# Reading, adding and storing seven of sixteen token groups during the last expert tiles of a fused perceiver layer

## The reference, cut to what matters

```python
logits = flat @ router_w.T
topk_scores, topk_idx = jax.lax.top_k(logits + router_bias, 2)
topk_scores = softmax(topk_scores)
hidden = silu(gate_all) * up_all                    # 16 experts of 128 hidden units
out = einsum('nk,nkd->nd', combine, down_all)       # two experts a token
out = out + (silu(flat @ sh_gate.T) * (flat @ sh_up.T)) @ sh_down.T
x = x + out
```

## Time and profile before

| | |
|---|---|
| median of 3 runs | 538.88 us (538.51 to 539.96) |
| profiled execution, its own time | 540.22 us |
| its span, first to last instruction | 538.5 us |
| PE / DVE / ACT / POOL busy | 498.2 / 399.3 / 200.1 / 198.0 us |
| chain that ended last | PE 70%, DVE 9%, DMA 8%, POOL 5% |
| mean granted clock of PE | 0.976 |

### The profile page before, as it was taken

The page is one execution under the profiler, slowest core; times in us unless marked ns, Lnnn a source line. Parts: engine busy times, 40 slices in busy tenths (PEclk is TensorE's granted clock), DMA queues, the critical chain, the costliest instruction groups (busy, mean ns, idle before and its releaser), DMA issues.

```text
span 538.5 us, 14453 instructions
## 1 busy us (share of the span) xinstructions
PE 498.2 (93%) x5012; PEld 348.7 (65%) x5013; DVE 399.3 (74%) x1068; ACT 200.1 (37%) x617; POOL 198.0 (37%) x314
## 2 busy tenths in 40 slices
PE   7988899999999999999989999999979899999950
PEld 7765566656666666666655667766735578888840
DVE  3699599999999999999653588888775325555545
ACT  2343323433223333333221366666341035555500
POOL 4000412212221112221222576766766616655620
PEclk9999999999999999999999999999998979999995
DMA  7999688877998888885215999710122245554249
GB/s 276 356 352 243 189 279 291 251 209 252 294 304 286 279 279 272 256 273 196 66 40 165 253 309 297 205 52 2 50 89 90 89 115 157 159 150 120 74 165 302
DMA packets 67348, 108.83 MB, mean 202 GB/s; under 512 B 8115, under 2 KB 49125, under 8 KB 67304
## 3 DMA queue, kind: packets, MB, share of 16 engines
q1 hardware_dynamic: 60888, 97.83, 58.6%
q0 software_dynamic: 3792, 8.43, 4.5%
q10 hardware_dynamic: 2624, 1.97, 1.2%
HBM read 85.31 MB, written 24.85 MB: 205 GB/s over the span
## 4 chain that ended last, share of the span: by engine, by line
PE 70%; DVE 9%; DMA 8%; POOL 5%; issue 4%; ACT 1%; SPq 1%; POOLq 0%; DVEq 0%; ACTq 0%
PE banks L1110 15%; PE banks L1134 15%; PE banks L1516 8%; DMA ring<-in_ctx_dram 5%; POOL rows_by_expert L727 4%; PE banks L1528 4%; PE banks L1122 3%; DVE ctxT L1638 3%; PE banks L1147 3%; PE banks L1069 2%; PE banks L1510 2%; DMA xn_all<-expert_out 2%; PE banks L1243 2%; PE banks L1295 2%; PE banks L1155 2%
## 5 line engine op out<-in xcount | busy, mean ns | idle before, releaser
L1638 DVE STREAM_TRANSPOSE ctxT<-ring 128x832 f32<-128x832 f32 x128 | 121.7, 1009 | 4.2 <-DMA ring<-in_ctx_dram 4.1
L1110 PE MATMUL banks<-ctxT,qT_all 32*64 32x416 f32 (+2 forms) x2048 | 93.9, 498 | 2.5 <-issue 2.1
L1134 PE MATMUL banks<-ring,prob 128*64 128x256 f32 (+1 forms) x832 | 93.6, 381 | 0.7 <-ACT prob L839 0.7
L1134 PEld LDWEIGHTS banks<-ring,prob 128*64 128x64 f32 (+1 forms) x832 | 58.6, 137 | 31.5 <-issue 4.2
L1110 PEld LDWEIGHTS banks<-ctxT,qT_all 32*64 32x64 f32 x2048 | 56.8, 131 | 31.2 <-issue 14.0
L638 POOL TENSOR_TENSOR var<-mv,eps 128x1 f32<-128x1 f32 x32 | 6.3, 196 | 168.6 <-DVE mv L1683 116.5
L761 POOL DMA_INDIRECT expert_out<-prob,dest x47 | 46.2, 984 | 41.6 <-DVE prob L2099 27.7
L852 ACT ACTIVATE prob<-banks,negmax 128x416 f32<-128x416 f32 (+2 forms) x80 | 41.1, 531 | 30.2 <-DVE negmax L1660 30.2
L1516 PE MATMUL banks<-ring,ctxT 128*128 x188 | 50.7, 394 | 0.1
L674 POOL TENSOR_TENSOR ctxT<-ctxT,k_mask 128x1088 f32<-128x1088 f32 x16 | 33.1, 2069 | 25.3 <-ACT ctxT L930 25.3
L839 ACT COPY prob<-banks 128x512 f32<-128x512 f32 x64 | 27.7, 514 | 38.0 <-PE banks L1122 37.9
(11 more groups left out here) (269 smaller groups left out, 940.5 us busy)
## 6 DMA issues: line engine op xcount, KB each, us to landing
ring<-in_ctx_dram SPq DMA_DIRECT2D x48, 1024.0 KB
qT_all<-q_by_pair SPq DMA_DIRECT2D x56, 128.0 KB, 8.9
rows_by_expert<-blank SPq DMA_DIRECT2D x8, 774.0 KB, 7.2
ctxT<-rows_by_expert SPq DMA_DIRECT2D x47, 129.0 KB, 2.1
mid<-stage SPq DMA_DIRECT2D x31, 128.0 KB, 2.3
ring<-in_ctx_dram SPq DMA_DIRECT2D x16, 130.0 KB
ctxT<-mid SPq DMA_DIRECT2D x16, 128.0 KB, 4.5
qT_all<-mid SPq DMA_DIRECT2D x16, 128.0 KB, 4.9
```

Source lines behind the costliest of these rows:

```text
L1110: last = pe.matmul(S[a][64 * b:64 * b + 64, 0:KW[a]], q_rep[mine, r, c, 64 * b:64 * b + 64], ctxT[mine, c, b, 0:KW[a]], start=c == 0, stop ...
L1134: last = pe.matmul(U[64 * b:64 * b + 64, 0:D], probT[0:rows, k, 64 * b:64 * b + 64], ring[0:rows, r, b, k, :], start=k == 0, stop=k == KT)
L1638: dve.transpose(ctxT[:, c].rearrange("p b (k j) -> p (b k) j", j=Q), ring[:, r].rearrange("p b k c -> p (b k) c")[:, :, columns(c):columns ...
```

## The change

Groups 0 to 6 are complete when the tiles of the first part have been sent, the first `FIRST_TILES` = 29 of the 47. SP now waits for those 29 sends behind the row load of tile 38 (`READ_AT`). It reads group g behind the row load of tile 38 + g, two DMAs of 128 rows each. DVE adds group g behind the result in turn 40 + g (`ADD_AT`, `group_added`). Behind the row load of tile 46 SP stores groups 0 to 3 and 4 to 6, when they have been added, and only then waits for all sends. The other nine groups are read, added and stored as before, in chunks of 4, 3 and 2. The loops over tiles end earlier (SP at tile 36, DVE at turn 40); the rest is written out. The four load semaphores become one, `weights_loaded`, and each wait asks for the sum of all loads up to its own.

```diff
-    CHUNKS = (4, 5, 5, 2)
+    CHUNKS = (2, 2, 3, 4, 3, 2)
+    SOON = 3
+    SOON_OUT = ((0, 4), (4, 7))
...
+    FIRST_TILES = (TOPK * PARTS[1] * P + NE * (P - 1)) // P
+    READ_AT = FIRST_TILES + 9
+    ADD_AT = READ_AT + 2
...
+    QK_LOADED = 16 * 2
+    REST_LOADED = QK_LOADED + 16 * 7
+    PREP_LOADED = REST_LOADED + 16 * (GB + 6)
+    EXPERTS_LOADED = PREP_LOADED + 16 * 3 * NE
...
-            pool.wait_ge(rest_loaded, 112)
+            pool.wait_ge(weights_loaded, REST_LOADED)
...
-            with sp.Fori(1, SLOTS // ROWS) as it:
+            def load_results(lo, hi, n):
+                for k in range(TOPK):
+                    sp.dma_start(y_all[k][:, lo:hi, :],
+                                 y_dram[k * TOK:(k + 1) * TOK, :].rearrange("(g p) c -> p g c", p=P)[:, lo:hi, :])\
+                        .then_inc(y_loaded[n], 16)
...
+            with sp.Fori(1, READ_AT // ROWS) as it:
...
-            for s in range(SLOTS // ROWS * ROWS, SLOTS):
+            for s in range(READ_AT // ROWS * ROWS, SLOTS):
                 sp.wait_ge(rowT_done, s - (ROWS - 1))
                 sp.wait_ge(dest_copied, s - (ROWS - 1))
                 load_rows(s, s % ROWS)
...
+                if s == READ_AT:
+                    results_sent(FIRST_TILES)
+                if READ_AT <= s < READ_AT + PARTS[1]:
+                    load_results(s - READ_AT, s - READ_AT + 1, chunk_of(s - READ_AT))
+            for lo, hi in SOON_OUT:
+                sp.wait_ge(mixed_ready, TOPK * hi)
+                store_out(lo, hi)
+            results_sent(SLOTS)
+            for n in range(SOON, len(CHUNKS)):
+                load_results(sum(CHUNKS[:n]), sum(CHUNKS[:n + 1]), n)
+            for n in range(SOON, len(CHUNKS)):
+                sp.wait_ge(mixed_ready, TOPK * (PARTS[1] + n - SOON + 1))
+                store_out(sum(CHUNKS[:n]), sum(CHUNKS[:n + 1]))
...
-            with dve.Fori(2, SLOTS // ROWS) as it:
+            def group_added(g):
+
+                n = chunk_of(g)
+                dve.wait_ge(y_loaded[n], 16 * TOPK * CHUNKS[n])
+                dve.wait_ge(shared_added, g + 1)
+                for k in range(TOPK):
+                    if k:
+                        dve.wait_ge(mixed_ready, TOPK * g + k)
+                    dve.tensor_tensor(x2_all[:, g, :], y_all[k][:, g, :], x2_all[:, g, :], ALU.add).then_inc(mixed_ready, 1)
+
+            with dve.Fori(2, ADD_AT // ROWS) as it:
                 for r in range(ROWS):
                     turn(it * ROWS + r, r, it)
-            for s in range(SLOTS // ROWS * ROWS, SLOTS):
+            for s in range(ADD_AT // ROWS * ROWS, SLOTS):
                 turn(s, s % ROWS, s // ROWS)
+                if ADD_AT <= s < ADD_AT + PARTS[1]:
+                    group_added(s - ADD_AT)
```

More of the change, by code:

```diff
@@ L405, in q_of, with chunk_of @@
             return q_dram[bass.ds(i, 1)].squeeze(0)
+        def chunk_of(g):
+            return next(n for n in range(len(CHUNKS)) if g < sum(CHUNKS[:n + 1]))
         def columns(c):
@@ L467, in _ @@
             load_x(4)
-            sp.dma_start(wv[:, :, :], t["L0_xattn_Wv"].rearrange("(k p) f -> p k f", p=P)).then_inc(rest_loaded, 16)
+            sp.dma_start(wv[:, :, :], t["L0_xattn_Wv"].rearrange("(k p) f -> p k f", p=P)).then_inc(weights_loaded, 16)
             store_q(0, DIRECT)
             for to, of in ((bv_b, "L0_xattn_bv"), (gamma_b, "L0_xattn_gamma"), (beta_b, "L0_xattn_beta")):
[L471 to L474, removed]
+                sp.dma_start(to[:, :], t[of].partition_broadcast(P)).then_inc(weights_loaded, 16)
+            sp.dma_start(bq2_col[:, :], t["L0_attn_b_q"].rearrange("(p a) -> p a", a=1)).then_inc(weights_loaded, 16)
+            sp.dma_start(bout_b[:, :], t["L0_attn_b_out"].partition_broadcast(P)).then_inc(weights_loaded, 16)
+            sp.dma_start(rbias_b[:, :], t["L0_ffn_router_bias"].partition_broadcast(P)).then_inc(weights_loaded, 16)
             def follow(i, r, stores=True):
@@ L555, in _, with store_out, results_sent @@
                 load_rows(s, s)
-            with sp.Fori(1, SLOTS // ROWS) as it:
+            def load_results(lo, hi, n):
[3 more added lines that the diff above has]
+                        .then_inc(y_loaded[n], 16)
+            def store_out(lo, hi):
+                for q in range(GB):
+                    sp.dma_start(out.rearrange("l (g q) c -> q l g c", q=GB)[q][:, lo:hi, :],
+                                 x2_all[NL * q:NL * q + NL, lo:hi, :]).then_inc(written, 16)
+            def results_sent(tiles):
+                for r in range(ROWS):
+                    sp.wait_ge(y_sent[r], 16 * ((tiles - r + ROWS - 1) // ROWS))
+            with sp.Fori(1, READ_AT // ROWS) as it:
                 for r in range(ROWS):
@@ L565, in _ @@
                 load_rows(s, s % ROWS)
[L566 to L580, removed]
+                if s == READ_AT:
[11 more added lines that the diff above has]
+                store_out(sum(CHUNKS[:n]), sum(CHUNKS[:n + 1]))
+            sp.wait_ge(written, 16 * GB * (len(SOON_OUT) + len(CHUNKS) - SOON))
         @block.gpsimd
@@ L940, in turn @@
                     act.copy(n2_second[:, bass.ds(i - 4, 1), 0:D].squeeze(1), n2_now).then_inc(n2b_ready, 1)
-            act.wait_ge(rest_loaded, 112)
+            act.wait_ge(weights_loaded, REST_LOADED)
             for i in range(6):
@@ L1016, in _ @@
             keep_awake(8)
-            pe.wait_ge(qk_loaded, 32)
+            pe.wait_ge(weights_loaded, QK_LOADED)
             for of, to in ((wq, 0), (wk, 1)):
@@ L1197, in _ @@
             turn_probs(1)
-            pe.wait_ge(rest_loaded, 112)
+            pe.wait_ge(weights_loaded, REST_LOADED)
             turn(2, 2, 0, back3=False, rows=2)
@@ L1215, in _ @@
             project(PAIRS - 1)
-            pe.wait_ge(prep_loaded, 16 * (GB + 6))
+            pe.wait_ge(weights_loaded, PREP_LOADED)
             pe.wait_ge(w_qp_ready, 1)
@@ L1549, in _ @@
             first, second = [None] + known(expert_first), known(expert_now)
-            pe.wait_ge(experts_loaded, 16 * 3 * NE)
+            pe.wait_ge(weights_loaded, EXPERTS_LOADED)
             pe.wait_ge(shared_added, 4 * LATE)
@@ L1764, in _ @@
             x_normed(3)
-            dve.wait_ge(rest_loaded, 112)
+            dve.wait_ge(weights_loaded, REST_LOADED)
             turn(2, 2, 0, back3=False, also=(4, 6))
@@ L2136, in _ @@
             shared_add(LATE)
-            for n in range(len(CHUNKS)):
+            for n in range(SOON, len(CHUNKS)):
                 results_added(n)
```

23 lines of the change are left out of this document (10 added, 13 removed).

## The result

The changed kernel takes 534.05 us (median of 9 runs, 533.32 to 537.23) against 539.0 for the kernel before (9 runs, 537.87 to 539.96). The ratio is 0.992, 95% interval 0.9902 to 0.9937, a gain of 3.4 to 5.3 us. The forecast was 533.3, a gain of 5.6: the right way and nearly the right size, a little more than the interval allows.

A forecast was written before the change was run, and what follows sets the result against it. PE paces the tiles; then a 21.2 us tail of reads, adds and stores overlaps nothing. Tail saving 5.7 less 0.1 for semaphore waits gives 5.6 us, from 538.88 to 533.3 us; range 532.1 to 535.8.

The forecast's parts named there:

- The place of the gain: Tail after the last tile: seven of sixteen groups leave it, 5.7 us less; PE's turns stay 1.63 us.
- Reads of the tail: Late chunks in the tail: second and third land at 524.7 and 526.1, before DVE wants them, at 379 GB/s.
- The bound that I gave this term: Tail: if the last two chunks' reads came as late as behind 5 groups, the gain would be 3.9 us.
- Adds and stores of the tail: Tail: adds end at 528.5; twelve stores, 0.50 us each without a break from 525.17, last issue at 530.7.
- the width line: DVE add time by width: 0.15 us plus 1.05 ns an element, so 0.95 us for 768 wide.
- SP in the tiles: Tiles 38 to 44: three issues take 1.2 of 1.63 us, 3.5 us of row-load lateness covered, DMA share 0.89.
- DVE in the tiles: Turns 40 to 46: two adds make DVE's turn 1.57 us, under 1.63; 0.1 us charged for semaphore waits.
- the rule of the Trainium skill: DVE in the tiles: a two-input add blocks until GpSimd's send is done; gain 5.3 us and not 5.6.
- DVE as the bound: Rival, last turns: adds slow the turn, 534.5 to 536.5 us, chance 0.13; nothing left at turn 2.4, chance 0.04.
- Late row loads: Rival, tiles: early reads delay row loads; decides from a 6 us landing, 542.0 at 11; chance 0.06, 0.04 slower.
- Early stores that stay on SP until after the last send: Rival, tile end: eight store issues after 517.17 cost up to 4.0 us, 537.3; chance 0.05.
- Merged semaphores: Load waits on one summed semaphore: claimed to cost nothing, with no issue moved.

The follow-up runs named there:

- reads: The changed kernel with the seven groups still read early, but added and stored in the tail: 535.37 us, ratio 0.9938, tail 17.6 us.
- rsplit: The changed kernel with ScalarE issuing the late reads of the second array, all stores on SP: 533.38 us, ratio 0.9899, tail 15.1 us.
- stores_late: The changed kernel with the eight early stores behind the six late reads on SP: 534.18 us, ratio 0.9917, tail 17.6 us.
- burst: The changed kernel with all early reads issued at once behind tile 38's row load, not two a turn: 537.83 us, ratio 0.9986.

## Why the prediction was right, and where it was off

- **The place of the gain.** Right: the tail fell by 4.8 us and PE's turns stayed at 1.63. The reads alone give 3.6 of it, by the tails.
- **Reads of the tail.** This is the term that was off. I took the late chunks as landing at 379 GB/s whatever stands behind them, 7.4 and 8.8 us into the tail. They landed at 9.0 and 10.4. The bound that I gave this term, a gain of 3.9, covered it, but I had reached that bound by more traffic ahead of the reads, and what came was less: 320 and 193 GB/s with reads outstanding. That it held is luck. The same reads are in at 8.9 in the run reads and at 8.7 in rsplit, whose tail is 15.1 (my sum: 15.5), so the sum was sound where the reads came at the rate that I took. What I left out is something in the changed kernel that delays them; the early stores on the same queue are the likely one, since reads lacks them (and the early adds), but how they would do it is not shown.
- **Adds and stores of the tail.** Adds took what the width line says (0.96 for 768 wide). They ended 12.3 us in, 1.1 later than summed, all of it the late landing. The last eight stores went out back to back, 0.46 us each, and the last started 14.3 us in (summed 13.4). I had SP issuing without a break from 525.17 on; it waited once more, since until 524.6 DMA was the bound, and SP's issues bound only from 526.6 on.
- **SP in the tiles.** Right: three issues a turn, no wait for it; row loads landed by 3.6 us at most, over the 3 that I had named as a sign but inside 5.5; the DMA share of 0.87 to 0.95 against 0.89 summed.
- **DVE in the tiles.** Right, the extra was 0 and not 0.1. The turn of 1.57 was 1.51. GpSimd's send never held an add, though they overlap by 0.2 us, so neither the 0.3 us by the rule of the Trainium skill nor my 0.07 a turn appeared.
- **The rivals.** DVE as the bound: adding as much again took the whole gain in the median, at a turn of 2.18 us, of which seven turns make 3.9 us. I had put the point where nothing is left at 2.4, since I took the gain as 5.6; the measured 5.0 would put it at 2.36, which the intervals do not tell from 2.18. Late row loads: forced by the burst, PE waited 3.3 us and lost 1.5 more at the lower clock, so the mechanism exists, and the change's spacing avoids it. The price that I gave it had no term for the clock. Early stores that stay on SP until after the last send: they did not, since they were issued by 511.1, 4.4 us before the late reads. What they would have cost is not shown; stores_late has them behind the reads and not in front of them.
- **Merged semaphores.** Right, nothing.

Open: why the engines move less while reads are outstanding, in the kernels that have the early stores and all late reads on SP's queue. No view here goes by single DMA engine.

## What to carry to other kernels

A rate read from one stretch need not hold for the shorter stretch that the change leaves behind, so look at the landing of each read in the new profile, and not only at the bytes. Here the reads were late on one queue that also had the early stores, and a second issuing queue for reads and stores paid (2.6 us of the tail), though a second queue paid nothing before. Work moved beside a pipeline should be summed as one turn of each engine that takes it up, and be spaced over the turns; the same reads in one burst cost nearly all they gained, once by PE's wait and once more by the clock behind it.

## What was not expected of the hardware

- 2.4 MB of reads from one issuing queue, which had eight stores just before, moved at 320 GB/s and less from 4.5 us into the tail (last in at 10.4 us); without those stores on one queue they were in at 8.9, and from two queues, at 381 up to 7.6 us into the tail, at 8.7.
- A send by GpSimd (an indirect write) took 1.21 us beside two-input adds of DVE, 0.98 elsewhere; the adds stayed at 0.42.
- After 3.3 us without work PE's granted clock was 0.50, and the next turn took 3.12 us instead of 1.63 (burst).
- 256-wide adds of 0.42 us that wait for nothing start 0.34 us apart.
